# Six gather passes of a graph network: the work on groups of 512 nodes moves inside the passes, to 33 places that read their group from a table

## The reference

```python
# L0: wx = x @ W.T + b;  wx * segment_sum(w**2 * wx[dst], src)
# L1: msg = concat([x[src], edge_attr]) @ W1 + b1
#     concat([x, segment_sum(msg, dst)]) @ W2 + b2
# L2, twice (relu between), w = edge_weight / deg[dst]:
#     segment_sum(w * x[src], dst) / max(deg, 1) @ Wl.T + x @ Wr.T
# L3, three times:
t = einsum('nd,kod->kno', h, W_et) + b_et          # 4 edge types
a = segment_sum(t[etype, src], dst)
h = gru_cell(a, h, W_ih, b_ih, W_hh, b_hh)
# then sigmoid(concat([h, x]) @ i_w.T + i_b) * (h @ j_w.T + j_b)
```

## Time and profile before

| | |
|---|---|
| median of 3 runs | 14,746.88 us |
| profiled execution | 14,774.5 us, span 14,772.8 us |
| mean granted TensorE clock | 0.75 |
| busy: PE, DVE, ACT, POOL | 61%, 45%, 9%, 66% of the span |
| transfers | 2,920 MB, 198 GB/s over the span |
| group work between and behind passes | 260, 89, 162, 246, 246 and 158 us |

### The profile page before, as it was taken

How to read it: one execution, slowest core, us unless ns; L and a number is a source line. 1 busy time by engine, 2 the same in 40 slices (tenths; PEclk the granted TensorE clock), 3 DMA queues, 4 the chain that set the end, 5 groups by cost and what they waited for, 6 DMA issues and landing times. The chain is left out here.

```text
span 14772.8 us, 170942 instructions
## 1 busy us (share of the span) xinstructions
PE 9067.6 (61%) x35200; PEld 6191.3 (42%) x35200; DVE 6699.5 (45%) x19880; ACT 1367.5 (9%) x4019; POOL 9809.0 (66%) x8999
## 2 busy tenths in 40 slices
PE   5344344444446666755555555678868777788877
PEld 3333333333433444643334333444444444444443
DVE  3333333333337777377767777522225222332225
ACT  1111111111110000100001000100001000100002
POOL 2777777777774777367775777277772777457771
PEclk6666666766768878666666666788879888888887
DMA  8999997777769999378877888499965999379972
GB/s 286 215 216 215 219 217 157 165 163 159 129 96 240 224 218 224 82 186 216 218 179 185 219 217 204 141 245 245 249 178 157 251 245 248 118 218 249 244 209 61
DMA packets 4163879, 2920.41 MB, mean 198 GB/s; under 512 B 448453, under 2 KB 3849154, under 8 KB 4163494
## 3 DMA queue, kind: packets, MB, share of 16 engines
q1 hardware_dynamic: 3613740, 2278.66, 57.3%
q0 software_dynamic: 518096, 623.51, 21.3%
q10 hardware_dynamic: 31722, 15.04, 0.4%
HBM read 2194.73 MB, written 750.41 MB: 199 GB/s over the span
## 5 line engine op out<-in xcount | busy, mean ns | idle before, releaser
L890 POOL DMA_INDIRECT ring<-t_types,stage x3456 | 3278.3, 949 | 1842.3 <-issue 1767.5
L1409 PE MATMUL bank<-ring 128*128 128x128 f32 x13824 | 2596.4, 348 | 2451.2 <-DMA ring<-t_types,stage 1039.1
L1409 PEld LDWEIGHTS bank<-ring 128*128 128x128 f32 x13824 | 2356.5, 252 | 3332.2 <-issue 3239.2
L890 POOL DMA_INDIRECT ring<-t_x,stage x2304 | 2239.9, 972 | 1142.0 <-issue 1078.6
L1805 DVE TENSOR_REDUCE work<-work 128x512 f32<-128x2048 f32 x588 | 2145.3, 3648 | 906.3 <-DMA work<-t_x 619.6
L1386 PE MATMUL bank<-work 128*128 128x512 f32 x4704 | 2389.4, 656 | 0.0
L849 POOL DMA_INDIRECT t_sums<-ring,stage x1152 | 1786.1, 1550 | 584.4 <-issue 265.8
L1791 DVE TENSOR_TENSOR acc<-acc,bank 128x128 f32 x1728 | 487.5, 282 | 3668.2 <-PE bank L1409 3639.5
L1386 PEld LDWEIGHTS bank<-work 128*128 128x128 f32 x4704 | 966.0, 217 | 1014.9 <-issue 1014.9
L890 POOL DMA_INDIRECT ring<-t_h,stage x1152 | 1093.9, 950 | 440.1 <-issue 410.8
L1300 PE MATMUL bank<-aux 128*128 128x128 f32 x2304 | 530.7, 403 | 1308.2 <-ACT aux L1013 1307.8
(11 more groups left out here) (264 smaller groups left out, 9565.1 us busy)
## 6 DMA issues: line engine op xcount, KB each, us to landing
work<-t_pairs SPq DMA_DIRECT2D x2352, 512.0 KB
t_pairs<-acc SPq DMA_DIRECT2D x272, 740.0 KB
work<-t_types SPq DMA_DIRECT2D x588, 256.0 KB
aux<-sorted_src SPq DMA_DIRECT2D x400, 256.0 KB, 5.7
t_pairs<-acc SPq DMA_DIRECT2D x78, 1300.0 KB
t_pairs<-acc SPq DMA_DIRECT2D x272, 370.0 KB
t_types<-ring SPq DMA_DIRECT2D x150, 512.0 KB, 2.8
ring<-t_types,stage POOLq DMA_INDIRECT x3456
```

The source lines that it names most:

```text
L890: pool.indirect_dma_start(msg[:, u, :], None, table, bass.IndirectOffsetOnAxis(ap=stage[:, u:u + 1], axis=0)).then_inc(slot_dma[u], 16)
L1409: mm = pe.matmul(bank[q][:, 0:P], msg[:, u, :], hot[:, u, :], start=k == 0, stop=k == K - 1)
```

## The change

**Steps inside the pass.** The turns of a pass are written out in pairs. Pair p holds six units, the two halves of three tiles in turn, and (from p = 1 to 33) step m = p − 1 of the group work: TensorE's parts follow the slots q0 to q3 of the pair's first turn, those of ScalarE and VectorE the slots of its second turn. A step reads the first node of its group from a table (`step_row`); where no further group is finished by then, it works on a dummy group of rows behind the real ones. Behind the pass `tail_steps` does 6 more steps, or 25 if the table says so. The table is computed at setup, from the sorted edges, on VectorE.

**Buffers.** All of a step's buffers (rows in, turned rows, copies, sums, result) are single. Unit blocks have two buffers, by half, where there were three; a tile's rows are loaded once for both halves, into one of three. The types table is two tables, used in turn.

**SP.** In each pair SP first loads the rows of step p − 1, then stores the result of step p − 2, then issues the six unit loads.

```diff
-NB = 3
+TILES = 3
+LEAD = ST // TILES
+DUE = SURE // 2
+STEPS = DUE - 1
+TAIL_STEPS = 6
...
+        def pairs_of_turns(eng, body):
+            body(0, NH * TILES)
+            body(1, NH * TILES)
+            with turns(eng, 2, LEAD) as p:
+                body(p, NH * TILES)
+            body(LEAD, LAST_UNITS)
+            body(LEAD + 1, 0)
...
+        def tail_steps(eng, total, step):
+            for j in range(TAIL_STEPS):
+                step(STEPS + j)
+            with eng.If(total - (STEPS + TAIL_STEPS) > 0):
+                with turns(eng, STEPS + TAIL_STEPS, STEPS + NG) as m:
+                    step(m)
```

SP's unit loads, the order within a pair, and a layer's load and store:

```diff
+            def unit_rows(ph, table, p, c):
+                half, tile = c % NH, c // NH
+                unit = p * (NH * TILES) + ((ph - 1) * UNITS + c)
+                wait(sp, types_summed if ph < 4 and half else dense_done,
+                     unit - 1 if not isinstance(p, int) or unit > 1 else 0)
...
+                    sp.dma_start(dense_b[:, half, k:k + 8, :], PAIR_BLOCKS[half][at, k:k + 8, int(ph in (2, 3)), :]
+                                 ).then_inc(dense_in[half], 16)
+                if half == 0:
+                    sp.dma_start(dense_t[:, tile, :] if ph > 3 else dense_x[:, tile, :], table[at, :]
+                                 ).then_inc(dense_x_in[tile], 16)
...
+            def stream_pass(ph, table, load, store):
+                def body(p, units):
+                    for a in range(2):
+                        if a == 0 and not (isinstance(p, int) and p == 0):
+                            load(p - 1)
+                            if not (isinstance(p, int) and p == 1):
+                                store(p - 2)
...
+                            for i in range(TILES):
+                                unit(i)
+                pairs_of_turns(sp, body)
...
+                tail_steps(sp, total, step)
+                store(total - 1, True)
+            def layer_pass(ph, k, loads, table, into):
+                def load(m):
+                    src_ = step_of(mybir.EngineType.SP, m, (NG - 1) * GN, step_src)
+                    wait(sp, step_free, before(total, k, m))
...
+                def store(m, last_=False):
+                    g = step_of(mybir.EngineType.SP, m)
+                    sp.wait_ge(step_rows, total * (k + 1) if last_ else before(total, k, m) + 1)
+                    sp.dma_start(node_rows_of(into, g), by_tile(s_res)).then_inc(step_out, 16)
```

TensorE's turns of a pair (the sixth unit follows the second turn), then VectorE's reduction of a unit and its turns of a pair:

```diff
+                    turn(p * 2, block, None if first else
+                         lambda q: parts[q](before(total, k, p - 1), g, done_by(ph, p - 1, False), before(total, min(k, 1), p - 1)))
+                    turn(p * 2 + 1, lambda i: block(TILES + i))
...
+                def type_sums(p, c):
...
+                    v.wait_ge(dense_in[half], p * (TILES * 32) + ((ph - 1) * ST * 32 + tile * 32 + 32))
+                    if not isinstance(p, int) or unit > 1:
+                        v.wait_ge(dense_done, unit - 1)
+                    v.tensor_reduce(dense_sum[:, half, :], dense_b[:, half, :, :].rearrange("p (k b) c -> p (b c) k", k=KT),
...
+                    turn(p * 2, first, block)
+                    turn(p * 2 + 1, False, lambda i: block(TILES + i),
+                         None if first else lambda q: parts[q](before(total, k, p - 1), g, before(total, min(k, 1), p - 1)))
```

Which part follows which slot on VectorE, and the new state with the wait of the next types rows:

```diff
+            gather_steps(1, 0, {1: l1_rows, 3: step_norm(4)}, low_of, None, features=True)
+            gather_steps(2, 1, {1: l2a_rows}, low_of, weight_of)
+            gather_steps(3, 2, {1: l2b_rows, 3: step_norm(5)}, low_of, weight_of)
...
+                    wait(v, types_out[0], i * 16 if n < 2 else total * 32)
...
+                    v.tensor_tensor(h, g_a, g_c, ALU.add)
+                    v.tensor_tensor(g_c, g_a, g_c, ALU.add).then_inc(h_ready, 1)
+            def types_add(hh):
+                    v.wait_ge(h_ready, i + 1)
+                    v.wait_ge(types_prod, i * 2 + (hh + 1))
```

More of the change, by code:

```diff
@@ L420, in wait, with node_rows_of, step_of, all_steps @@
                 eng.wait_ge(s_, n)
[L422 to L427, removed]
+        def pairs_of_turns(eng, body):
[5 more added lines that the diff above has]
+            body(LEAD + 1, 0)
+        def node_rows_of(t, node, cols_=slice(0, A)):
+            return t[bass.ds(node, GN), :].rearrange("(a p) f -> p a f", a=A)[:, cols_, :]
+        def step_of(eng, m, top=NG * GN, row=None):
+            return loaded(eng, cols(step_row if row is None else row, m, 1), 1, top, "the kernel writes the first nodes of its groups")[0]
+        def all_steps(eng):
+            eng.wait_ge(regs_ready, 2)
+            return loaded(eng.engine, step_total[0:1, 0:1], 1, STEPS + NG, "the kernel writes one of two numbers",
+                          STEPS + TAIL_STEPS)[0]
+        def before(total, k, m):
+            return total * k + m if k else m
+        def tail_steps(eng, total, step):
[4 more added lines that the diff above has]
+                    step(m)
+        def done_by(ph, m, tail_):
+            return ph * ADDS if tail_ else m * (2 * NQ) + ((ph - 1) * ADDS + NQ + 1)
         def cols(t, start, n):
@@ L595, in dense_turns @@
[L595 to L608, removed]
@@ L616, in features_in @@
[L616 to L625, removed]
-            dense_pass(3, H1)
-            pass_rows(p_l2b, p_l2b.var, [(xin, H1), (yin, X2)], to_table(p_l2b, X3), ph=3)
@@ L1422, in no_turn @@
+                pairs_of_turns(pe, body)
+                turn(SURE - 1)
                 def no_turn(t, n):
@@ L1445, in _, with step, turn_step, part @@
-            ahead(p_l1, l1_prod)
-            def l2_steps(d, wl, wr):
-                def prod(at):
-                    par = at.par
-                    pe.wait_ge(d.free, at.g + 1)
+                def step(m):
+                    g = step_of(mybir.EngineType.PE, m)
+                    for q in sorted(parts):
+                        parts[q](before(total, k, m), g, done_by(ph, m, True), before(total, min(k, 1), m))
+                tail_steps(pe, total, step)
+            def turn_step(per):
+                def part(i, g, done, normed_):
+                    pe.wait_ge(step_in, (i + 1) * 16 if per == 1 else normed_ * 32 + 32)
+                    wait(pe, step_free, i)
+                    for a in range(A):
+                        mm = pe.transpose(bank[6][:, a * P:(a + 1) * P], s_xin[:, a * D:(a + 1) * D], ident[:, :])
+                    mm.then_inc(step_turned, 1)
+                return part
@@ new lines, in gate_sums @@
+            def gate_sums(i, g, done, normed_):
+                a, h = cols(acc, g, GN), cols(aux, g, GN)
+                pe.wait_ge(added, done)
+                if gate_sums.n < 2:
+                    wait(pe, types_rows, i * 2)
+                else:
+                    pe.wait_ge(types_rows, total * 4)
+                    pe.wait_ge(h_ready, i)
+                for c in range(2):
+                    pe.matmul(bank[6 + c][:, :], wT[:, W_IH + c, :], a, start=True, stop=False)
+                    mm = pe.matmul(bank[6 + c][:, :], wT[:, W_HH + c, :], h, start=False, stop=True)
+                mm.then_inc(gate_prod, 1)
@@ L1946, in _ @@
-            v.sem_inc(p_l2a.free, 2)
-            def l2a_step(at):
-                g, par = at.g, at.par
-                v.wait_ge(p_l2a.prod, g + 1)
-                wait(v, p_l2a.rows, g - 1)
-                combine(p_l2a, par, g)
-                if not (at.known and at.pair == 0):
-                    v.wait_ge(p_l2a.st[par], at.pair * 16 + p_l2a.st_before[par])
-                v.tensor_scalar(res[:, par, :], z[:, par, :], 0.0, None, ALU.max).then_inc(p_l2a.rows, 1)
-            linked(l2a_step, 2)
```

637 lines of the change are left out of this document (381 added, 256 removed).

## The result

The changed kernel takes 14,652.42 us (median of 4 runs, 14,646.16 to 14,655.32), the kernel before beside it 14,746.64: a ratio of 0.9936, 95% interval 0.9919 to 0.9954. It is 94 us faster. The forecast was 14,890, slower, at 0.62. The profiled execution (14,650.9, span 14,649.3) is like the median; that of before stood 28 us above its own, so the spans of the two profiles differ by 123.5 us.

A forecast was written before the change was run, and what follows sets the result against it. POOL's gather issue was taken to bound the passes; +220, +150, +10, +80 and +5 inside them, +8 setup and −330 behind them gave +143, 14,917, or 14,890 on the median's scale; range 14,450 to 15,170.

The forecast's parts named there:

- Rival A: Passes 1 to 6: two unit buffers suffice, passes keep their length, only gaps fall; 14,425 us, chance 0.27.
- I take the low clock: Serial steps behind the passes: TensorE at its low clock, 27 us a state step; gaps sum to −330 us.
- the 19.4 reckoned at full clock: State steps behind passes 4 and 5: a serial step takes 19.4 us with TensorE at full clock.
- the −500 at full clock: Gaps behind all six passes: alternative sum of about −500 us, were TensorE at full clock there.
- After pass 2: 16 us a step: Behind pass 2: serial steps whose next load waits for the combine; 110 us against 89, a loss of about 20.
- 17.5 after pass 3: Behind pass 3: 17.5 us a serial step, 122 us against 162, saving 40.
- Where the clock falls for part of a pair up to 42. I take 41.3: Inside passes 4 and 5: TensorE's time per pair with a step, 41.3 us; +40 us a pass.
- Rival B: Passes 4 and 5: TensorE bounds them, its clock falling behind each state wait; pair 46 us, whole 15,200, chance 0.12.
- some eight handovers: Pairs of pass 3: handovers between engines at 0.2 us each add 1.6 us, making a pair 47 us.
- the chain's 45.4: Pass 3: serial waits, loads, reductions and step work from one norm to the next, 45.4 us a pair before handovers.
- Setup, +8: Setup: the step table's 20 small linked operations, a matmul and register loads add 8 us (3 to 15).
- C: Cancellation: 4 us stalls a pair in passes 1 and 3 offset the gaps; within about 50 us of 14,747, chance 0.10.

The follow-up runs named there:

- both edits: Changed kernel with SP's store between the turns' unit loads and half-0 loads released by the reduction (passes 1 to 3): 14,372.4 us, 0.973 of before.
- The filled versions: Matmuls of constants added behind the passes to the changed kernel (16,326.8 us, 1.0099) and to the version with both edits (15,951.4 us; 14,282.9 on another chip).

## Why the prediction was wrong

**What was right.** POOL's issue as the bound of a pass; 39 steps with 6 of them behind each pass; a stretch of passes 1 and 3, and of them alone, from two waits for unit data in each pair, the first unit's behind SP's store and the third's behind a buffer; the load time of 7 us; the low clock behind pass 1 (0.51) and the length of that stretch (121 put, 115 measured). The two edits confirm the two waits: of the 177 us in pass 3, 95 go with SP's order and 71 with the release. Rival A (two buffers suffice) failed as an account of the changed kernel, though the run with all steps behind shows that it holds where VectorE has room. The rule of the Trainium skill, "Trainium Kernel Development and Optimization", section "Best Practices", to double-buffer so that transfers overlap compute, was not at fault by itself: two buffers hid the loads of pass 3 with the steps behind it (1449 us) and with the steps inside and both edits (1455), but not with SP's order and the release as they stood (1622).

**What failed** is the sum, 266 us too high on the profiled execution: 128 in the gaps (the first two points below), 58 in passes 4 and 5, 43 in pass 3, and 37 in setup and the other passes together.

- *"I take the low clock"* for all steps behind the passes: −330 for a measured −458. For the state steps it was wrong: 27 us a step were put, and 21 to 23 measured after passes 4 and 5, nearer to the 19.4 reckoned at full clock. With pass 6 that is 67 of the 128 us. VectorE and TensorE behind pass 4:

```profile
11191.17 0.75 DVE L2218 SCALAR_TENSOR_TENSOR work<-bank,gru_b,work 128x512 f32<-128x512 f32 x1 [9.63 <-PE bank L1626]
...
11196.33 3.78 PE L1636 MATMUL bank<-wT,work 128*128 128x512 f32 x4 [5.25 <-DVE work L2225]
...
11201.56 1.98 PE L1636 MATMUL bank<-wT,work 128*128 128x512 f32 x4 [1.45 <-DVE work L2235]
...
11206.14 1.02 PE L1618 MATMUL bank<-aux,wT 128*128 x2
...
11212.31 0.75 DVE L2218 SCALAR_TENSOR_TENSOR work<-bank,gru_b,work 128x512 f32<-128x512 f32 x1 [7.37 <-PE bank L1626]
...
11217.47 3.52 PE L1636 MATMUL bank<-wT,work 128*128 128x512 f32 x4 [5.25 <-DVE work L2225]
...
11233.18 0.75 DVE L2218 SCALAR_TENSOR_TENSOR work<-bank,gru_b,work 128x512 f32<-128x512 f32 x1 [7.37 <-PE bank L1626]
```

Steps start 21.1 and 20.9 us apart (11191.17, 11212.31, 11233.18). Four records of the products for the next types table (L1636) take 3.78 us behind a wait of 5.25, and 1.98 the next time; the gates (L1618, two records in 1.02 us) go at that faster rate too. The clock of the stretch is 0.79: the forecast had carried one row of a slow unit after a wait to a whole phase. The Trainium skill, "TensorE: Matmul & The Clock Gate", section "HAM oscillation — how this bites in real kernels", has each burst of matmuls behind a DMA wait start at the slow clock again; in the state stretches the trace agrees for the first burst of a step and not for the rest of it, and the stretches after passes 1 and 2 (0.51, 0.60) do stand at or near the low level. The filled versions took another 52 us off the whole (58 to 62 in the stretches of the profiles), which makes some −510 to −520 for the gaps; the −500 at full clock that stood beside the choice was nearer than the −330.
- *"After pass 2: 16 us a step"*, and 17.5 after pass 3, were mis-sized whatever the clock: 55 of the 128 us. VectorE's combine (L2165) and the first product (L1586) behind pass 2:

```profile
7797.68 1.12 DVE L2165 TENSOR_SCALAR work<-bank,rdeg 128x128 f32<-128x128 f32 x4 [4.92 <-PE bank L1587]
...
7805.83 0.80 PE L1586 MATMUL bank<-wT,s_acc 128*128 128x128 f32 x2 [1.28 <-ACT work L1229]
...
7808.98 0.63 PE L1587 MATMUL bank<-wT,work 128*128 128x128 f32 x2
...
7809.76 1.13 DVE L2165 TENSOR_SCALAR work<-bank,rdeg 128x128 f32<-128x128 f32 x4 [9.07 <-PE bank L1587]
...
7820.95 1.12 DVE L2165 TENSOR_SCALAR work<-bank,rdeg 128x128 f32<-128x128 f32 x4 [8.57 <-PE bank L1587]
```

11.2 to 12.1 us a step, although the clock is low: the products run from 7805.83 to 7809.6, 3.8 us. The prediction gives no terms for its 16, so which part of it was too long can't be told; a step after pass 1, at a low clock too, took 15.3. After pass 3 a step took 12.9 (run with all steps behind).
- *"Where the clock falls for part of a pair up to 42. I take 41.3"* for passes 4 and 5: +80 for a measured +22. The steps' matmuls closed TensorE's idle time (busy 1278 of 1454 us in pass 4, for 1113 of 1444), and the clock rose from 0.84 to 0.96. The eight-record units cost less for it. Their group on the page before and after:

```profile
L1386 PE MATMUL bank<-work 128*128 128x512 f32 x4704 | 2389.4, 656 | 0.0
...
L1505 PE MATMUL bank<-work 128*128 128x512 f32 x4704 | 2149.0, 600 | 84.2 <-DMA work<-t_pairs 58.9
```

That is 240 us less in all. Without steps inside, the clock was 0.87 with the same buffers, so the steps raised it. Rival B, and the 42 in the forecast, had the sign of this effect wrong.
- *The pairs of pass 3*, where "some eight handovers" were put on top of the chain's 45.4: 47 for a measured 45.5, 43 us in all. From the norm's end to the third unit's reduction the trace has 20.6 us where the chain had 19.9, from there to the next norm's end 24.7 where it had 25.5 without handovers. That the sum came out like the chain without them is in part luck: one half was too short, the other too long.

Setup, +8 for −14, is not shown to be a gain: the first gather of pass 1 started at 4563.7 to 4599.3 us in the runs of this study, so 20 us there mean nothing.

The sign of the change hung on the difference of two large sums, +465 in the passes and −330 behind them in the forecast, +349 and −458 measured, and all four points above erred the same way. Two slips in the rivals' sums changed nothing: B sets +390 against +60 where the forecast had +80 (its next sum uses 80), and C adds 18 for passes 2 and 6, which had 15. The chance of 0.62 for slower was too firm for that.

## What to carry to other kernels

Work that was moved under a bound engine cost here what its waits pushed back in the queues it shares, not its own time (163 us more of VectorE's work in pass 3 cost 10 us once the waits were gone). Look in SP's queue for a store, with its wait for the step's last result, ahead of a load that the next unit needs, and put the load first; and free a buffer at its last reader, here the reduction, not at the product behind it. Two buffers that cost nothing with the reducing engine busy for 1072 us of a pass of 1445 cost 12% of the pass with 1235, and 0.7% once both were done. Where a phase is at the low clock, two or three wide matmuls of constants for each group are worth a trial; here they shortened one phase of the old kernel by 59 us, and took 52 us off the new one. Try them: why they help is not shown.

## What the runs showed of the hardware that was not expected

- Added TensorE work made the clock rise: pass 4, 1113 us busy at 0.84, 1278 us busy at 0.96 with 660 matmul records more.
- A phase with TensorE busy 90% of the time, in products of 128 columns (some of 33 rows) and of one column, ran at 0.50; with two 512-column ones behind each group's it ran at 0.93, with TensorE busy 89% of the time.
- One chip ran the kernel before in 16,173 us and the two others in 14,747 to 14,771; the passes of the version with both edits were 17 to 21% longer there and the stretches between them the same. Its gain over the kernel before was 2.7% on one chip and 1.1% on that one: a comparison that is close holds for the chip it was made on.
